# The skip term of a state-space scan moved from VectorE to ScalarE and GpSimd

## What is computed

```python
xBC = silu(conv1d(hidden @ in_proj_w.T, 4 taps) + conv_b)     # x, B, C
D_res = D[None, None, :, None] * x                            # the skip term
Y_diag = einsum('bhcij,bcjhd->bcihd', (C·B) * L, x * dt)
Y_off  = einsum('bckhn,bchdn,bhck->bckhd', C, state, state_decay)
y = (Y_diag + Y_off) + D_res
y = y * silu(gate)
y = group_rmsnorm(y) * norm_w @ out_proj_w.T
```

## Time and profile before

| what | value |
|---|---|
| median of 3 runs | 2067.46 us (2064.92 to 2067.75) |
| the profiled execution's own time | 2064.27 us |
| its span in the profile | 2062.3 us |
| TensorE busy | 1977.5 us, 96% of the span |
| VectorE busy | 1644.3 us, 80% |
| ScalarE busy | 958.1 us, 46% |
| GpSimd busy | 571.5 us, 28% |
| mean granted TensorE clock | 0.988 of full speed |

### The profile page before, as it was taken

One profiled execution on the slowest core, in us unless ns is written; L12 is line 12 of the kernel. 1 busy time (PEld: TensorE's weight loads), 2 busy tenths in 40 slices (PEclk: granted clock), 3 DMA queues, 4 the chain that ended last, 5 costly groups with the idle time before them and its releaser, 6 DMA issues.

```text
span 2062.3 us, 27185 instructions
## 1 busy us (share of the span) xinstructions
PE 1977.5 (96%) x9904; PEld 1388.3 (67%) x9904; DVE 1644.3 (80%) x2367; ACT 958.1 (46%) x1327; POOL 571.5 (28%) x467
## 2 busy tenths in 40 slices
PE   6899978999999999999999999999999999999987
PEld 4677756666676767666666676666666666666654
DVE  4888634878787877878788989898989888898976
ACT  2323336445454545454545454544545454545431
POOL 2864633222222222222222222222222222222200
PEclk9999989999999999999999999999999999999998
DMA  2222343222232323232323242323223232323220
GB/s 82 57 69 61 102 156 82 56 91 82 69 110 63 106 67 111 68 111 63 106 63 115 72 147 77 111 73 100 69 74 98 75 109 77 111 73 105 78 66 17
DMA packets 84995, 176.38 MB, mean 86 GB/s; under 512 B 13936, under 2 KB 20208, under 8 KB 84736
## 3 DMA queue, kind: packets, MB, share of 16 engines
q1 hardware_dynamic: 59904, 108.06, 17.7%
q10 hardware_dynamic: 24960, 66.60, 10.7%
HBM read 164.39 MB, written 10.22 MB: 85 GB/s over the span
## 4 chain that ended last, share of the span: by engine, by line
PE 64%; DVE 14%; issue 7%; ACT 1%; POOL 0%; DVEq 0%; POOLq 0%; ACTq 0%
PE bank L854 31%; PE bank L946 17%; DVE conv L1179 5%; PE bank L885 4%; DVE conv L1183 4%; PE bank L872 4%; PE bank L907 3%; PE bank L897 2%; PE bank L914 2%; ACT conv L1033 1%; DVE xdec L1272 1%; DVE ya L1244 1%; DVE ys L1295 1%; DVE xdt L1269 1%; DVE M L1287 1%
## 5 line engine op out<-in xcount | busy, mean ns | idle before, releaser
L854 PE MATMUL bank<-xnp,wxp 128*128 128x512 f32 x3456 | 866.1, 403 | 23.9 <-DVE conv L1183 11.4
L854 PEld LDWEIGHTS bank<-xnp,wxp 128*128 128x128 f32 x3456 | 639.3, 189 | 184.9 <-POOL wxp L1139 31.2
L1139 POOL TENSOR_TENSOR wxp<-wxs,wxp 128x512 fp32r<-128x512 f32 x288 | 382.9, 1332 | 1158.2 <-ACT wxp L1026 1158.2
L946 PE MATMUL bank<-wos,gT 128*128 128x512 f32 x1024 | 451.9, 594 | 2.6 <-DVE gT L1260 2.6
L1179 DVE SCALAR_TENSOR_TENSOR conv<-bank,cws,conv 128x509 f32<-128x509 f32 (+2 forms) x480 | 358.1, 746 | 22.2 <-ACT conv L1033 10.8
L946 PEld LDWEIGHTS bank<-wos,gT 128*128 128x128 f32 x1024 | 190.2, 191 | 218.2 <-issue 215.4
L1033 ACT ACTIVATE conv<-bank,cbs,cws 128x512 f32<-128x512 f32 x160 | 124.3, 777 | 304.3 <-PE bank L854 304.3
L1026 ACT ACTIVATE wxp<-wxs 128x512 fp32r<-128x512 f32 x288 | 178.9, 621 | 17.7 <-PEq L842 14.2
L1287 DVE SCALAR_TENSOR_TENSOR M<-M,gb 128x1024 f32<-128x1024 f32 x128 | 169.9, 1328 | 7.5 <-DVE gb L1279 0.5
L1041 ACT ACTIVATE gT<-bank 128x512 f32<-128x512 f32 x128 | 76.3, 596 | 196.6 <-PE bank L854 195.9
L1057 ACT ACTIVATE xT<-conv 128x512 f32<-128x512 f32 x160 | 100.1, 625 | 113.2 <-DVE conv L1183 85.1
(11 more groups left out here) (138 smaller groups left out, 2140.0 us busy)
## 6 DMA issues: line engine op xcount, KB each, us to landing
wxs<-wp SPq DMA_DIRECT2D x288, 256.0 KB, 2.7
wos<-wout ACTq DMA_DIRECT2D x64, 512.0 KB, 5.7
ecs<-ecs_scratch ACTq DMA_DIRECT2D x112, 256.0 KB, 4.0
wxs<-w SPq DMA_DIRECT2D x56, 256.0 KB, 2.6
state_scratch<-S SPq DMA_DIRECT2D x8, 512.0 KB, 2.9
S<-state_scratch SPq DMA_DIRECT2D x8, 512.0 KB, 3.7
out<-acc SPq DMA_DIRECT2D x8, 256.0 KB, 3.1
tab_scratch<-tabs ACTq DMA_DIRECT2D x2, 768.0 KB, 4.4
```

The source lines that it names most:

```text
L854: last = pe.matmul(bank(k), wxp[:, k % 2, a, kk, :], xnp[:, half, b, kk, :], start=kk == 0 and a + b == 0, stop=kk == KT - 1 and a == 1)
L946: last = pe.matmul(Y[:, 512:512 + HID], gT[u % 2][:, t, tokens(q)], wos[:, t, :], start=t == 0, stop=t == XT - 1)
L1139: pool.tensor_tensor(wxp[:, k % 2, 1], wxs[:, k % AHEAD], wxp[:, k % 2, 0], ALU.subtract).then_inc(w_lo, 1)
```

## The change

VectorE no longer makes D times x. `decay_off` multiplies bank Z into the `ecs` tile in place and no longer touches `ya`. A new `skip(q)` on ScalarE writes D times x of the cell into `ya` with 8 copies of 128x128 with a scale; it is called for q+1 behind `leave_bank(ks[3])` of cell q. A new `join(q)` on GpSimd adds `ecs` to `ya` (128x1024); it is called for q+1 between `low` of the fourth tile and `rnorm(q)`. `load_ecs` waits for `join` instead of `decay_off` and stands behind `load_row` instead of at the cell's start.

```diff
 # ScalarE
     def load_ecs(q):
-        act.wait_ge(u1_d, done(q - 1))
+        act.wait_ge(u2_d, done(q - 1))
+    def skip(q):
+        u, _, g, c = place(q)
+        act.wait_ge(y_d, done(q))
+        if c == 0:
+            act.wait_ge(silu_d, done(u * WT + XT))
+        for t in range(XT):
+            last = act.activation(ya[:, t, :], xT[u % 2][:, 2 + t, tokens(q)], ACT.Copy, scale=dch[:, g, t:t + 1])
+        last.then_inc(skip_d, 1)
...
+    skip(0)
     for n in range(PIECES):
         norm_out(0, n)
     for q in range(CELLS):
...
-        load_ecs(q + 2)
...
         load_row(q + 2)
+        load_ecs(q + 2)
...
         for k in ks[3:4]:
             leave_bank(k)
+        if more:
+            skip(q + 1)
 # GpSimd
+    def join(q):
+        pool.wait_ge(u1_d, done(q + 1))
+        pool.wait_ge(skip_d, done(q + 1))
+        if fresh(q):
+            pool.sem_inc(u2_d, 1)
+        else:
+            pool.tensor_tensor(ya[:], ya[:], ecs[:, q % 2], ALU.add).then_inc(u2_d, 1)
...
         for k in tiles_of(q)[:4]:
             low(k + 2)
+        if q + 1 < CELLS:
+            join(q + 1)
         rnorm(q)
 # VectorE
     def decay_off(q):
-        dve.wait_ge(y_d, done(q))
-        dve.tensor_tensor(ya[:].rearrange("p t i -> p (t i)"), Z[:],
-                          ecs[:, q % 2].rearrange("p t i -> p (t i)"), ALU.mult).then_inc(u1_d, 1)
+        past = ecs[:, q % 2].rearrange("p t i -> p (t i)")
+        dve.tensor_tensor(past, Z[:], past, ALU.mult).then_inc(u1_d, 1)
-    def skip(q):
-        ...
-        for t in range(XT):
-            x = xT[u % 2][:, 2 + t, tokens(q)]
-            if fresh(q):
-                last = dve.tensor_scalar(ya[:, t, :], x, dch[:, g, t:t + 1], None, ALU.mult)
-            else:
-                last = dve.scalar_tensor_tensor(out=ya[:, t, :], in0=x, scalar=dch[:, g, t:t + 1], in1=ya[:, t, :],
-                                                op0=ALU.mult, op1=ALU.add)
-        last.then_inc(u2_d, 1)
...
-        skip(q)
         add_diagonal(q)
```

More of the change, by code:

```diff
@@ L711, in scan @@
                              "y_s", "r_v", "acc_d"))
-        y_rn = sem("y_rn")
+        y_rn, skip_d = sem("y_rn"), sem("skip_d")
         tb, X, Y, Z = banks
@@ L995, in _ @@
         def _(act):
-            for s in (w_hi, tap_d, silu_d, z_d, e_a, e_b, y_sq, wo_n):
+            for s in (w_hi, tap_d, silu_d, z_d, e_a, e_b, y_sq, wo_n, skip_d):
                 act.sem_inc(s, CREDIT)
@@ L1132, in _ @@
         def _(pool):
-            for s in (w_lo, y_rn):
+            for s in (w_lo, u2_d, y_rn):
                 pool.sem_inc(s, CREDIT)
@@ L1153, in _ @@
                 low(k + 2)
+            join(0)
             for q in range(CELLS):
@@ L1162, in _ @@
         def _(dve):
-            for s in (conv_step, conv_d, s_mul, s_add, u1_d, u2_d, u3_d, y_d, x_dt, x_dec, g_cp, m_mul, y_s, r_v, acc_d):
+            for s in (conv_step, conv_d, s_mul, s_add, u1_d, u3_d, y_d, x_dt, x_dec, g_cp, m_mul, y_s, r_v, acc_d):
                 dve.sem_inc(s, CREDIT)
```

## The result

The changed kernel takes 2086.57 us (median of 6 runs, 2084.54 to 2088.68), the kernel before 2066.74 us in its 6 runs: ratio 1.0097, 95% interval 1.0084 to 1.0110. It is 19.8 us slower; the prediction said 18.6 us slower, 2086.1.

The account below looks back on a forecast made before the run. TensorE bounds the first half; in the second it waits for GpSimd's `low`. Eight units at 0.9 + 1.35 us give 18, plus 0.6 at the start: 18.6 us on 2067.46 makes 2086.1 us, range 2069 to 2096.

Parts of the forecast that it names:

- What bounds the kernel: TensorE busy throughout the first half; in the second half it waits for the end of GpSimd's `low`, 2.3 us a unit.
- upper bound: Most that a faster VectorE could bring in the second half: 2.3 us in each of 8 units, 18.4 us.
- What is removed: VectorE's skip operations, eight in each of 56 cells, 129.4 us busy: nobody waits for them, value 0.
- ScalarE: Eight added copies a cell, 2.5 us; moved table-load issues make ScalarE's work until the skip 0.27 us later at c=2.
- The join: GpSimd's added 128x1024 addition takes 2.36 us, holding a VectorE halo operation and `weigh` in second-half cells c=0 and c=2.
- The steps: Second half: late halo operations caught by `low` delay TensorE 0.9 us in c=1 and 1.35 in c=3, 18 us over 8 units.
- harder hit: Rival: c=1 and c=3 both pay the larger step, or late `acc` also holds `diagonal`; 29.4 us more, 2097 us; chance 0.08.
- The start: First cell: skip(0) ahead of the weight scaling delays the tap and TensorE's ks[2]; 0.6 us more, once.
- faster: Rival: second-half waits were VectorE's load after all; 2049 us if all vanish, 2058 more likely; chance 0.05.
- no hit: Rival: slower ScalarE copies put the join behind `weigh`'s start, so it waits instead; 2067 to 2070 us; chance 0.12.
- milder hit: Rival: shifts 0.2 to 0.4 us smaller, c=1 pays 0 and c=3 0.9; 7.8 us more, 2075 us; chance 0.17.

Follow-up runs that it names:

- Run 5: Kernel before the change, with the three border operations of each second-half convolution placed behind its three taps: 2048.99 us, ratio 0.9925.
- Run 1: Changed kernel with the join's addition on VectorE, ahead of add_diagonal, instead of GpSimd; ScalarE keeps its new work: 2066.37 us, ratio 1.0000.
- run 7: Changed kernel with the join behind rnorm on GpSimd and the second-half border operations behind the taps: 2050.20 us, ratio 0.9927.
- run 6: Changed kernel with the second-half border operations behind the taps, join left in its place: 2068.45 us, ratio 1.0016.
- run 2: Changed kernel with the join still on GpSimd but behind rnorm, beside VectorE operations that read PSUM: 2065.57 us, ratio 0.9997.
- run 8: Changed kernel with two GpSimd memsets of 128x1024 in place of the join, leaving out the skip term and the state's part of y: 2066.34 us, ratio 1.0002.
- run 4: Changed kernel with the join split into two GpSimd instructions of 128x512: 2065.27 us, ratio 0.9997.
- run 3: Changed kernel with only load_ecs moved back to the start of the cell: 2073.01 us, ratio 1.0033.

## Why the prediction was right

**What bounds the kernel.** Right: TensorE in the first half, GpSimd's `low` in the second. Run 5 shows the second: moving VectorE's border operations out of `low`'s way, without taking any work off VectorE, gave 16 of the 18.4 us named as the upper bound.

**What is removed is worth 0.** Right. Run 1 puts 1.2 us a cell back and run 7 takes it away again; neither shows.

**ScalarE.** Eight copies were put at 2.5 us and took 2.44. The table load was to come 0.27 us later; it came 0.39 us later, the time that ScalarE stood for the issues.

**The join.** Put at 2.36 us, took 2.41 (1414.46), with a median of 2.40; its mean of 2.54 has waits in it. It met the one-column operation, as forecast, and `weigh` started as the join ended.

**The steps.** In c=1 the forecast was 0.9 us, in c=3 0.9 or 1.8, counted as 1.35. By TensorE's waits c=3 grew from 0.22 to 0.87 + 1.11 = 1.98 us, so 1.8 was paid: the first border operation was caught, by 0.07 us (1421.59 against 1421.52). This is the term that was mis-sized, by 0.4 us in seven units, 2.9 us. The eighth, the first with border operations, paid only 0.19 us in c=3, because no `low` ran beside that convolution; a loss in all eight was counted. So c=3 came to 12.5 us where 10.8 was counted, and part of the closeness of the total is two misses of opposite sign. For c=1 the rows of the changed kernel are these:

```profile
1366.14 1.97 PE L907 MATMUL bank<-M,xdt 128*64 128x128 f32 x32 [0.28 <-DVE acc L1316]
...
1367.28 1.27 POOL L1152 TENSOR_TENSOR wxp<-wxs,wxp 128x512 fp32r<-128x512 f32 x1 [1.52 <-ACT wxp L1026]
1367.48 1.08 DVE L1208 SCALAR_TENSOR_TENSOR conv<-halo,cws,conv 128x2 f32<-128x2 f32 x1
...
1369.62 1.64 PE L854 MATMUL bank<-xnp,wxp 128*128 128x512 f32 x6 [0.97 <-DVE conv L1208]
```

The second border operation is the caught one, 0.2 us behind `low`'s start, and the wait grew from 0.41 to 0.28 + 0.97 us, 0.84 more.

**What came out differently.** `diagonal`'s wait for `acc`, which I named only under the harder hit, is real in both places (0.87 and 0.28 us). It adds little, by the order of the rows: VectorE's convolution does not wait for `diagonal` and ends where it ends, so ks[2] would have been held until then anyway. No run isolates this. And run 6 shows that a step is no condition of the cost: without it the same late start costs about as much.

**The start.** I put it at 0.6 us. In the two profiles the first `gram` transpose of the scan already stands 1.9 us later after the change (351.61 against 349.74), ahead of the first `skip` (352.71); over the ten profiled executions of this case it lies between 349.1 and 352.8 us, and both ends are variants of the changed kernel. Of the profile's 22.0 us these 1.9 are not the change's. Behind it, ks[2] of the first cell moved from 361.11 to 363.29, 2.18 us, so the start proper costs 0.3 us. With 12.5 us for c=3 and 6.7 for c=1 that makes 19.5 of the 19.8 us measured.

**The rules that were named.** The Trainium skill (SBUF — State Buffer, section "SBUF: two separate sides") has the shared ports as an exclusive lock, and a VectorE operation with two SBUF inputs contends for it only against a GpSimd operation that reads SBUF. The traces agree: held until the end of the join (1.92 us for 0.21), not held with an input in PSUM (run 2, 1.21 us), not held beside memsets (run 8, 0.21 us), and GpSimd held in its turn (run 4, 2.36 us for 1.29). The warning in the Trainium skill (Perfetto Trace Analysis, section "Optimizing Scalar/DVE Operations") that moving work between VectorE and GpSimd might not help was the one to heed. Its first clause, moving work off a saturated VectorE, would have given the wrong sign to whoever took 80% busy for saturated.

The rivals "faster", "no hit" and "milder hit" fall with the rows above. What stays open is why one cell c=2 (at 1398.21) lost its usual 0.4 us wait in the changed kernel's profile; it is one of 31, and lies in the window of 112.0 us shown above.

## What to carry to other kernels

Before work is moved off a busy engine, ask who waits for that engine at that place: here nobody did, and 115 us less of a busy VectorE were worth nothing. Before work is moved to GpSimd, list VectorE's operations with two SBUF inputs that can run at that moment: here each of them, down to one column, stood for the rest of the GpSimd instruction. What helped here was to place GpSimd's operation beside VectorE's PSUM operations (run 2), to cut it in two (run 4), and to gather the small two-input operations behind the taps (run 5); the last made the kernel before 0.75% faster.

## What the runs showed of the hardware that I had not expected

- A VectorE operation on one column took 1.92 us behind a GpSimd tensor_tensor of 2.41 us, against 0.21 us free and 0.21 us beside a GpSimd memset of 0.95 us. In the changed kernel's whole trace 95 border operations started while a GpSimd tensor_tensor ran, and each of them ended 13 to 24 ns behind it; the 218 taps on the bank that started so took 0.747 us in the mean, as did the 132 that met none.
- When the first half of a split join ended, VectorE's waiting operation and the next one behind it both went before GpSimd's second instruction (2.36 us instead of 1.29). So here VectorE's queue kept its turn against a GpSimd instruction that followed at once.
- The effect of a delay can come in steps: 0.4 us less shift in c=0 and c=2 of the second half (run 3) brought 13.6 us, because a GpSimd operation at a fixed place either catches a small operation or does not. With the small operations out of its way (run 6) a delay of about that size reached TensorE without a step.
- Two DMA issues on ScalarE's queue, 1.10 us together, delayed the table load behind them by 0.39 us, the part that the running exponential (1406.45 to 1407.47) did not cover.
